# Attention with a routed expert layer on one core: each head's stack of q and k loaded as two halves of 1024 columns instead of four quarters of 512

## What is computed

```python
qkv = x @ Wqkv.T + bqkv
q, k, v = jnp.split(qkv, 3, axis=-1)          # then (b, 16 heads, t, 32)
q = _rope(q)
k = _rope(k)
att = jnp.einsum('bhqd,bhkd->bhqk', q, k) * scale
att = jnp.where(causal, att, -jnp.inf)
att = jax.nn.softmax(att, axis=-1)
y = jnp.einsum('bhqk,bhkd->bhqd', att, v)
```

## Time and profile before

| what | before |
|---|---|
| median of three runs | 4234.07 us |
| the profiled execution, its own time | 4235.04 us |
| span of its trace | 4233.2 us |
| mean granted TensorE clock | 0.948 of full |
| PE busy | 3848.5 us (91%) |
| POOL busy | 2774.7 us (66%) |
| DVE busy | 2753.7 us (65%) |
| ACT busy | 1805.8 us (43%) |
| DMA queue of SP | 485.62 MB, 38.3% of 16 engines' span |

### The profile page before, as it was taken

The page is one execution under the profiler, slowest core; times in us unless marked ns, Lnnn a source line. Parts: engine busy times, 40 slices in busy tenths (PEclk is TensorE's granted clock), DMA queues, the critical chain, the costliest instruction groups (busy, mean ns, idle before and its releaser), DMA issues. The chain is left out here.

```text
span 4233.2 us, 81098 instructions
## 1 busy us (share of the span) xinstructions
PE 3848.5 (91%) x21344; PEld 2333.0 (55%) x21344; DVE 2753.7 (65%) x5889; ACT 1805.8 (43%) x3526; POOL 2774.7 (66%) x2251
## 2 busy tenths in 40 slices
PE   5989999987999999879899999879899999859998
PEld 2755554456744554457655554457555544547776
DVE  3767677466757767476667776567676774646655
ACT  1345655423355555332355555233455554311111
POOL 3768788824678878616578888427687887115554
PEclk8989999998999999989899999889899999979999
DMA  6543334252533343434433333425333332349997
GB/s 209 177 127 89 94 101 107 80 185 99 179 92 102 87 112 87 133 124 146 143 92 102 99 100 111 153 83 181 116 91 91 101 106 87 102 137 259 257 258 188
DMA packets 305135, 549.12 MB, mean 130 GB/s; under 512 B 59572, under 2 KB 99636, under 8 KB 301492
## 3 DMA queue, kind: packets, MB, share of 16 engines
q1 hardware_dynamic: 283192, 485.62, 38.3%
q0 software_dynamic: 21504, 58.40, 5.9%
HBM read 311.86 MB, written 174.85 MB: 115 GB/s over the span
## 5 line engine op out<-in xcount | busy, mean ns | idle before, releaser
L1141 ACT ACTIVATE Pt<-PS 128x512 f32<-128x512 f32 (+3 forms) x2560 | 1205.4, 544 | 1005.5 <-PE PS L1334 558.5
L1006 POOL TENSOR_TENSOR Sm<-Pt 128x512 f32<-128x512 f32 (+3 forms) x960 | 1027.7, 1077 | 356.2 <-ACT Pt L1141 337.9
L1653 DVE TENSOR_REDUCE part<-PS 128x1 f32<-128x512 f32 x1536 | 997.4, 684 | 295.9 <-PE PS L1311 291.6
L1311 PE MATMUL PS<-QK 96*128 96x512 f32 (+3 forms) x2560 | 1017.1, 418 | 56.7 <-DVE part L1649 23.9
L1334 PE MATMUL PS<-QK 97*128 97x512 f32 (+3 forms) x2560 | 991.9, 408 | 41.1 <-DMA QK<-mT 18.6
L1358 PE MATMUL PS<-Pt,V 128*32 128x512 f32 (+3 forms) x5120 | 874.0, 554 | 44.7 <-POOL Sm L1006 44.2
L1362 PE MATMUL PS<-Sm,onesv 128*32 128x512 f32 (+3 forms) x1920 | 822.6, 534 | 0.0
L1334 PEld LDWEIGHTS PS<-QK 97*128 97x128 f32 x2560 | 485.9, 193 | 481.9 <-issue 328.5
L1006 POOL TENSOR_TENSOR Sm<-Sm,Pt 128x512 f32<-128x512 f32 (+1 forms) x640 | 712.6, 1113 | 50.2
L1649 DVE CUSTOM_DVE_ANT_0 PS<-PS,consts 128x128 f32<-128x128 f32 (+3 forms) x1024 | 502.4, 495 | 346.8 <-PE PS L1311 344.0
L1311 PEld LDWEIGHTS PS<-QK 96*128 96x128 f32 x2560 | 496.6, 195 | 245.4 <-DVE part L1653 120.1
(11 more groups left out here) (169 smaller groups left out, 4907.9 us busy)
## 6 DMA issues: line engine op xcount, KB each, us to landing
QK<-qkd SPq DMA_DIRECT2D x720, 128.0 KB, 3.1
qkd<-st SPq DMA_DIRECT2D x64, 1024.0 KB, 4.5
Wg<-wgu SPq DMA_DIRECT2D x48, 768.0 KB, 4.9
o<-od SPq DMA_DIRECT2D x448, 64.0 KB, 2.0
W<-wd SPq DMA_DIRECT2D x3, 6144.0 KB, 21.6
Wd<-wdn SPq DMA_DIRECT2D x48, 384.0 KB, 5.8
xin<-x SPq DMA_DIRECT2D x16, 1024.0 KB, 7.8
vd<-vst SPq DMA_DIRECT2D x16, 1024.0 KB, 6.2
```

Of the source, the lines that this page charges most:

```text
L1006: nc.gpsimd.tensor_tensor(total, of[0][:, first:CH] if i == 1 else total, of[i][:, first:CH], ALU.add).then_inc(sum_done, 1)
L1141: nc.scalar.activation(Pt[:, t % NPT, first:CH], S2[t % NS2][:, first:CH], ACT.Exp, scale=SCALE).then_inc(exp_done, 1)
L1311: mm(s1[:, 0:w], QK[0:3 * HD, hh % 2, 0, qb * P:(qb + 1) * P], QK[0:3 * HD, hh % 2, 1, c * CH:c * CH + w], start=True, stop=True).then_inc ...
L1653: v.reduce_max(part[:, qb, cc:cc + 1], s1[:, 0:w], AX.X).then_inc(s1_dve, 1)
```

## The change

The transfers of heads 1 to 15 now cover 1024 columns each: `stack_half(hh, half)` issues three transfers of 256 KB, and is called twice, so six in place of twelve. Each half has one semaphore, and PE waits for it at query blocks 0 and 8 in place of 0, 4, 8 and 12. Head 0 keeps its quarters, under semaphores of its own, `qk_first`. The wait values follow from that: an even buffer now gets seven loads a batch through `qk_in[0]`.

```diff
--- before.py
+++ after.py
@@ -537,7 +537,8 @@
         st_out = [sem("st_out0"), sem("st_out1")]
         v_out = [sem("v_out0"), sem("v_out1")]
         v_in = [sem("v_in0"), sem("v_in1")]
-        qk_in = [[sem("qk_in%d%d" % (i, j)) for j in range(NCH)] for i in range(2)]
+        qk_first = [sem("qk_first%d" % j) for j in range(NCH)]
+        qk_in = [[sem("qk_in%d%d" % (i, half)) for half in range(2)] for i in range(2)]
         s1_ready = sem("s1_ready")
         s1_dve = sem("s1_dve")
         max_all = sem("max_all")
@@ -691,18 +692,26 @@
                 load_input(1)
                 sp.dma_start(bvg[:, :], bv.rearrange("g p -> (g p)").partition_broadcast(P)).then_inc(bv_in, 16)
 
-                def stack(hh, j, parts):
+                def stack_first(j, parts):
 
                     cols = slice(j * CH, (j + 1) * CH)
                     for blk, pair in enumerate((parts[:, 0::2], parts[:, 1:3], parts[:, 0::3])):
-                        sp.dma_start(QK[blk * HD:(blk + 1) * HD, hh % 2, :, cols].bitcast(F32), pair).then_inc(qk_in[hh % 2][j], 16)
+                        sp.dma_start(QK[blk * HD:(blk + 1) * HD, 0, :, cols].bitcast(F32), pair).then_inc(qk_first[j], 16)
+
+                def stack_half(hh, half):
+
+                    g, h = divmod(hh, GH)
+                    cols = slice(half * (T // 2), (half + 1) * (T // 2))
+                    parts = qkd[b, g, h * HD:(h + 1) * HD, :, cols]
+                    for blk, pair in enumerate((parts[:, 0::2], parts[:, 1:3], parts[:, 0::3])):
+                        sp.dma_start(QK[blk * HD:(blk + 1) * HD, hh % 2, :, cols].bitcast(F32), pair).then_inc(qk_in[hh % 2][half], 16)
 
                 def store_parts(n):
 
                     j, g = divmod(n, NG)
                     wait_apart(sp, q_lo, NCK * b + n + 1)
                     if g == 0:
-                        stack(0, j, st[n % 2][0:HD].bitcast(F32))
+                        stack_first(j, st[n % 2][0:HD].bitcast(F32))
                     sp.dma_start(qkd[b, g, :, :, j * CH:(j + 1) * CH], st[n % 2][:, :, :].bitcast(F32)).then_inc(st_out[n % 2], 16)
 
                 def store_values(j):
@@ -791,8 +800,8 @@
 
                         wait_apart(sp, s2_ready, NPT_B * b + NTILE * (hh - 1))
                     if hh < H:
-                        for j in range(NCH):
-                            stack(hh, j, qkd[b, g, h * HD:(h + 1) * HD, :, j * CH:(j + 1) * CH])
+                        for half in range(2):
+                            stack_half(hh, half)
                     max_row(hh - 1, 1)
                     if hh >= 2:
                         move(hh - 2, NCH - 1)
@@ -1114,7 +1123,7 @@
 
                         act.wait_ge(st_out[n % 2], ONE + 16 * (NCK // 2 * b + n // 2))
                         if g == 2:
-                            act.wait_ge(qk_in[0][j], ONE + 48 * (H // 2 * b + 1))
+                            act.wait_ge(qk_first[j], ONE + 48 * (b + 1))
                         nc.scalar.activation(st[n % 2][:, 0::2], t1[:, n % 2], ACT.Copy).then_inc(q_hi, 1)
                     elif kind == "copy":
                         _, hh, j = step
@@ -1305,9 +1314,13 @@
                     elif kind == "max":
                         _, hh, i = step
                         qb, c, w = TILES[i]
-                        if qb % TPC == 0 and c == 0:
-
-                            pe.wait_ge(qk_in[hh % 2][qb // TPC], ONE + 48 * (H // 2 * b + hh // 2 + 1))
+                        if hh == 0 and qb % TPC == 0 and c == 0:
+
+                            pe.wait_ge(qk_first[qb // TPC], ONE + 48 * (b + 1))
+                        elif qb % (NT // 2) == 0 and c == 0:
+
+                            turn_of = hh // 2 + 1 if hh % 2 else hh // 2
+                            pe.wait_ge(qk_in[hh % 2][qb // (NT // 2)], ONE + 48 * ((H // 2 if hh % 2 else H // 2 - 1) * b + turn_of))
                         mm(s1[:, 0:w], QK[0:3 * HD, hh % 2, 0, qb * P:(qb + 1) * P], QK[0:3 * HD, hh % 2, 1, c * CH:c * CH + w],
                            start=True, stop=True).then_inc(s1_ready, 1)
                     elif kind == "row":
```

## The result

The changed kernel takes 4291.22 us (median of four, 4282.28 to 4307.59) against 4234.24 us of the kernel before: a ratio of 1.0138, 95% interval 1.0106 to 1.017. It is 57 us slower, where 4234.4 with a range from 4222 to 4252 was forecast. The profiled execution took 4288.05 us, 53.0 more than the one of before.

What follows compares the result with a forecast made beforehand. PE, busy for 91% of the span, was taken to bound the kernel; 4235.0 (profiled execution) - 12.7 (saved on SP) + 11.3 (first products) + 1.7 (clock) = 4235.3, or 4234.4 us on the median's scale, range 4222 to 4252.

Steps and rivals of the forecast that it cites:

- What bounds the kernel: In the streams of heads, PE, busy 91% of the span: nearly every microsecond it loses or saves goes to the end.
- What the first product loses: Even heads 2 to 12, four batches: the first half lands 0.65 us later than the quarter, a loss of 11.3 us.
- "slower" rival: At the even heads' first products the first half comes 1.1 us late, giving 4251 us; chance 0.25.
- The rule that the prediction quotes: A transfer takes about 2.0 us plus its bytes at 436 GB/s; the first products' loss would be 3.7 us.
- "faster" rival: The halves land nearly as early, 0.3 us of delay, no clock fall, 3.5 us saved a batch: 4224 us; chance 0.20.
- What is saved on SP: At head 1, six issues take about 3.9 us, not 7.79, so PE gets the maxima earlier: 12.7 us over four batches.
- the forecast's later bound: At head 1 the maxima queue behind 1.57 MB of stack, whose last bytes land at about 258.9, issues starting at 250.0.
- Head 14 and the odd heads: Head 14's delay hides before 1.89 us of waiting for POOL; odd heads have 0.7 us or more in hand: no cost.
- The clock: Behind longer waits in heads 2, 6 and 10 PE's clock falls to half: one fall, 1.7 us, bounds none and four.
- The burst that does not shrink: Rival: at SP, six issues last 7.8 us as before, first half 1.6 us late, 4270 us; chance 0.05.
- The signs to look for: In the changed kernel's profile: SP's burst about 3.9 us, PE's stack wait some 20 us, maxima's wait 2 to 6.

Runs made afterwards that it cites:

- the benches: Two kernels computing nothing of the block, SP alone loading 1.5 MB bursts: the change's load landed after 9.4 us, 128 channels into 128 partitions after 6.3 us.

## Why the prediction was wrong

*What bounds the kernel.* Right. Both ends of the change were where it put them, and what it moved there went to the end nearly one for one.

*What the first product loses.* This is the step that failed. It took the arrival of the first half at 5.05 us after the first issue, 0.65 later than the quarter's; it was 6.2, 1.8 later. The prediction had the right figure in its hands: 384 KB more at the 250 GB/s of the earlier trace rows are 1.57 us. It took 0.4 off for idle engines, rounded the rest down to make a bound of 1.1, and then went by a row of another load, `Wg<-wgu`, 768 KB in 4.9 us. That load goes to 128 partitions; the benches show that such loads can run faster than those into 32. The 0.75 of DMA share in a burst of small transfers was no reserve of a quarter: with full queues the loads of the change moved at 235 GB/s with a share of 1.00, only 26% over the 187 of before. With 1.8 in place of 0.65, the prediction's own sum gives 24 x 1.8 - 3.64 - 0.74 = 39 us for the even heads 2 to 12, where it had 11.3. In the trace 41.9 us of waiting stand there, 1.5 of them from before. That the two are so near is in part luck: head 6 alone has 12.0 of them, from an arrival of 7.6 to 8.2 us. Its "slower" rival named this mechanism with 1.1 us and gave 4251 us; the sign was right, but of the 57 us it had 17.

The rule that the prediction quotes ("DMA: Bandwidth & Descriptors", anatomy of one DMA) is given by the Trainium skill as a fit to transfers issued from GpSimd, and these are issued from SP. Its 0.30 us for a 256 KB transfer in place of 128 KB stands against 1.8 measured for the third of three, and the "faster" rival that it would have borne out did not come.

*What is saved on SP.* The issues shrank as forecast, 7.79 to 4.08 us. The 3.2 us of the first batch were 0.8: the maxima landed 10.1 us after the first issue, and the forecast's later bound, 8.9, was itself too early. Same cause, the rate. That the row of waits fell from 18.6 to 6.9 us is mostly head 1's own first product being later by 1.8 us and so taking that part of the wait upon itself (2.44 + 1.80 us after, 0.60 + 4.47 before, 0.83 us less). Over the four batches head 1's waits for its stack (2.2 before, 10.1 after) and for maxima sum to 20.8 us before and 17.0 after: 3.8 us saved, where 12.7 was forecast.

*Head 14 and the odd heads.* Head 14's delay was hidden as forecast: its four waits for POOL, 1.9 us each, are gone, and 7.0 us of waiting for the stack stand in their place. The odd heads from 3 on, with 0.7 us and more in hand, were to lose nothing, and wait 4.4 us.

*The clock.* One fall was forecast, with four as the bound. In four windows, each from a stream's first "score" product to its last, PE is busy for 16.4 us more in all (the sums of the windows, first before, then after):

```profile
sum 2446.40, PE 2317.47; mean PE 579.37
...
sum 2505.20, PE 2333.87; mean PE 583.47
```

Outside the streams it is busy for 5.4 us less. Behind fourteen of the waits for stacks of heads 2 to 14 the granted clock is 0.50 for 3.4 us, beginning within 1.5 us of that product, as in the two windows shown above for heads 6 and 8. At the prediction's price of 1.7 us each that would be 24 us; some falls that the streams had before are gone, 30 being left where 22 were. So the term was too small by about a factor of ten, and it follows from the same late arrival. That all of the 16.4 us is clock is an estimate from these counts, not a run.

With this the whole is accounted for: 40.4 us in the even heads 2 to 12, 4.4 in the odd ones, 0.7 less in head 14 and 3.8 less in head 1, 2.2 more of waiting for POOL outside head 14, and 11.0 of busy time make 53.5.

*The burst that does not shrink.* Wrong in its reason, since the issues did shrink. That its 4270 us comes nearest of all to the 4291 is luck, though what it feared of the queue is true of the engines behind it.

*The signs to look for.* The text called itself wrong if the wait for the stack passed 28 us or the maxima still arrived at 259 or later. Both came: 63.4 us, and 259.3. The 256 KB loads were to land in 3.5 us (median); they took 5.6. The 6.8 us that it starts from were read as PE's, and are those of two engines: 3.7 us are PE's.

## What to carry to other kernels

A DMA share of 0.75 in a burst of small transfers isn't a quarter in reserve; price added bytes in front of a wait at the rate of that very pattern (its partitions, its source rows), and take rows of other loads only as a bound. A piece that a waiting engine needs first should be small and stand alone; coarser transfers are for what is needed later, and even there half the issues won nothing (nine transfers for twelve, 4233.5 us against 4234.7). A small transfer behind a large load came with that load's last bytes, so change its place in the queue: that won 20 us here, and fewer issues before it 0.8 us a batch or nothing.

## What the runs showed of the hardware

Loads into 32 partitions ran at 223 to 235 GB/s with the engines' share at 0.98 to 1.01, in rows of 4 or 8 KB, while 128 partitions from 128 channels reached 375 GB/s in the same kernel. A busy share is therefore no measure of the rate: 235 and 375 GB/s stood at 1.00 and 0.93. A 4 KB transfer issued 4.3 us after the start of a 1.5 MB load let PE go on 5.8 us after its issue, and 2.9 us when it was issued after 8.0. And PE's clock fell to half for 3.4 us behind single waits of 1.28 us (head 8) and 3.35 us (head 6), but not behind one of 1.35 us (head 4), so the length of the one wait does not tell alone.
